# Six edge passes of a graph-transformer kernel: four bf16 products that nobody reads ahead of each chunk's product, sixteen ahead of the first

## The reference, cut to what matters

```python
# layers 0 and 2: attention over edges
msgs = xl[src] * alpha[:, :, None]
out = jax.ops.segment_sum(msgs, dst, num_segments=n)
# layer 1, twice
msg = ew[:, None] * h[src]
agg = jax.ops.segment_sum(msg, dst, num_segments=x.shape[0])
# layer 3, three times (widths 256, 512, 256)
msg = h[src] * norm[:, None]
agg = jnp.zeros_like(h).at[dst].add(msg)
```

## The kernel before

| pass | stands for | columns | beside it |
|---|---|---|---|
| a0 | layer 0 attention | 264 | `l0_queries` |
| c1a | layer 1, first | 256 | layer 1 mixing |
| c1b | layer 1, second | 256 | nothing |
| a2 | layer 2 attention | 272 | `l2_mix` |
| d3a | layer 3, first | 256 | `l3_mix` |
| d3c | layer 3, second | 512 | nothing |
| d3e | layer 3, third | 256 | nothing |

## Time and profile before

### The profile page before, as it was taken

One profiled execution on the slowest core, in us unless ns is written; L12 is line 12 of the kernel. 1 busy time (PEld: TensorE's weight loads), 2 busy tenths in 40 slices (PEclk: granted clock), 3 DMA queues, 4 the chain that ended last, 5 costly groups with the idle time before them and its releaser, 6 DMA issues.

```text
span 7906.2 us, 73457 instructions
## 1 busy us (share of the span) xinstructions
PE 5426.0 (69%) x20758; PEld 3443.5 (44%) x20758; DVE 4236.9 (54%) x12574; ACT 1138.5 (14%) x2552; POOL 3801.9 (48%) x3736
## 2 busy tenths in 40 slices
PE   4302566655876677776887776666678777777698
PEld 3102453325743333335776443454443224333587
DVE  8713676675254444445288676865533664444411
ACT  1001241111210010002242122110010001000222
POOL 3773026652556636652502666027643664666133
PEclk9998778876977875567988988788889999555799
DMA  2101243334733323334742334023334664333465
GB/s 63 39 3 30 81 134 92 92 71 127 200 93 92 91 66 91 92 74 136 187 135 83 90 88 109 9 62 89 89 72 119 184 181 126 92 92 87 130 196 173
DMA packets 345017, 801.98 MB, mean 101 GB/s; under 512 B 96963, under 2 KB 196807, under 8 KB 331845
## 3 DMA queue, kind: packets, MB, share of 16 engines
q0 software_dynamic: 202752, 491.35, 24.2%
q1 hardware_dynamic: 141872, 305.94, 12.4%
HBM read 722.42 MB, written 77.80 MB: 101 GB/s over the span
## 4 chain that ended last, share of the span: by engine, by line
PE 41%; DVE 16%; DMA 10%; issue 9%; POOL 6%; another core or an unknown queue 4%; DVEq 1%; ACT 1%; POOLq 0%; SPq 0%; PEld 0%; PEldq 0%; ACTq 0%
PE bank L2138 20%; DMA arena<-TAB,arena 6%; POOL arena L2121 5%; PE bank L1402 4%; PE bank L1388 4%; DVE arena L2182 4%; PE bank L341 3%; DVE arena L2171 2%; DVE arena L2440 1%; PE bank L1615 1%; PE bank L1604 1%; DVE arena L2161 1%; DMA SUM<-arena 1%; DVE arena L228 1%
## 5 line engine op out<-in xcount | busy, mean ns | idle before, releaser
L2138 PE MATMUL bank<-arena 128*125 128x256 f32 (+3 forms) x5824 | 2658.8, 565 | 1183.8 <-DMA arena<-TAB,arena 262.7
L2121 POOL DMA_INDIRECT arena<-TAB,arena x2080 | 1991.5, 957 | 1672.0 <-DMA TAB<-arena 652.8
L2138 PEld LDWEIGHTS bank<-arena 128*125 128x125 f32 x5824 | 1186.8, 243 | 2603.2 <-issue 921.6
L2182 DVE TENSOR_TENSOR arena<-bank,arena 125x256 f32 (+3 forms) x2912 | 1351.4, 464 | 1524.5 <-PE bank L2138 966.3
L2121 POOL DMA_INDIRECT arena<-TABa,arena x832 | 865.0, 1040 | 1162.4 <-DVEq L141 774.4
L2161 DVE TENSOR_SCALAR arena<-arena 128x125 f32<-128x125 f32 x2080 | 616.9, 297 | 275.1 <-PE bank L2138 140.6
L1739 POOL DMA_INDIRECT REC<-arena x400 | 427.8, 1070 | 230.4 <-issue 121.6
L1343 POOL DMA_INDIRECT SUM<-arena x192 | 307.4, 1601 | 459.1 <-DVE arena L1553 391.6
L341 PE MATMUL bank<-arena 128*125 128x256 f32 (+4 forms) x1600 | 455.7, 433 | 89.2 <-DVE arena L2278 24.2
L1388 PE MATMUL bank<-arena 128*128 128x256 f32 x2048 | 465.3, 383 | 7.0 <-DVE arena L1541 4.8
L1402 PE MATMUL bank<-arena 128*128 128x256 f32 x2048 | 463.9, 383 | 0.0
(11 more groups left out here) (506 smaller groups left out, 5651.6 us busy)
## 6 DMA issues: line engine op xcount, KB each, us to landing
arena<-L_ffn_pack SPq DMA_DIRECT2D x32, 2054.0 KB
arena<-L_ffn_pack SPq DMA_DIRECT2D x64, 1026.0 KB
arena<-TAB,arena POOLq DMA_INDIRECT x2080
arena<-SLR SPq DMA_DIRECT2D x52, 512.0 KB, 3.7
arena<-DLR SPq DMA_DIRECT2D x52, 512.0 KB, 4.8
arena<-TABa,arena POOLq DMA_INDIRECT x832
arena<-L_ffn_b SPq DMA_DIRECT2D x96, 128.0 KB
arena<-LROW SPq DMA_DIRECT2D x20, 610.4 KB
```

The lines of the kernel that those rows point to most:

```text
L2121: e.indirect_dma_start(out=m.G[k % m.ring][:, 0:m.width], out_offset=None, in_=m.table[:, :], in_offset=bass.IndirectOffsetOnAxis(ap=eidx[ ...
L2138: e.matmul(ps[0:P, 0:m.full], m.S[k % SRING], m.G[k % m.ring], start=True, stop=True).then_inc(*put("pass_p", m.g, "summed", k))
L2182: e.tensor_tensor(o, banks.of(m.g, "added", k)[0:P, 0:m.full], o, ALU.add).then_inc(*put("pass_v", m.g, "added", k))
```

## The change

In six of the passes (all but the one of 512 columns) TensorE now computes further products between its wait for the bank and its wait for the chunk's matrix and rows: sixteen for the first chunk, four for each other. They are bf16, 128 rows by 256, 248 or 240 columns, each with its own loading of 128x128 weights; both operands are the bytes of constants that never change (`ident`, `ones` and what follows, read as bf16). They write the columns of the same bank that the chunk's fp32 product leaves free, which nobody reads, and signal no semaphore. In d3c no column is free, and nothing is added.

```diff
+    STEADY, FIRST = 4, 16
+    keepw, keepx = at(K0, 128, p=128, dt=BF16), at(K0, 256, p=128, dt=BF16)
+
+    def keep_pe(e, m, ps, k):
+
+        w = min(256, 512 - m.full)
+        if w < 128:
+            return
+        for _ in range(FIRST if k == 0 else STEADY):
+            e.matmul(ps[:, m.full:m.full + w], keepw, keepx[:, 0:w], start=True, stop=True)
+
     def pass_pe(e, m, steps=None, room=None):
         upto = beside(steps)
         for k in range(KC):
...
             if before:
                 e.wait_ge(*of(*before))
+            keep_pe(e, m, ps, k)
             e.wait_ge(*of(m.g, "onehot", k))
             if m.heads:
                 e.wait_ge(*of(m.g, "extra", k))
```

## The result

The changed kernel takes 7248.52 us (median of 6 runs, 7222.65 to 7261.45) beside 7198.32 us for the kernel before on the same chip (6 runs, 7190.85 to 7215.84). The ratio is 1.0065, 95% interval 1.005 to 1.0079: 36 to 57 us slower, about 47. The forecast was 7226 us, with a range of 7150 to 7320.

What follows compares the result with a forecast made beforehand. The prediction took GpSimd's gathers, 1.25 us a chunk, to bound the passes, not TensorE. Terms +20 (a2), +10 (d3a), +5 (a0), -5 (behind the passes) made +30 on the median 7196: 7226 us, range 7150 to 7320.

Steps and rivals of the forecast that it cites:

- The clock: In all six changed passes TensorE would run at the high clock, as in d3c at 0.96; 0.9 or more expected.
- Rival 4: The clock stays low: 241 us more in each of c1b and d3e, 7680 us or above; chance 0.05.
- c1b and d3e, cost 0: In c1b and d3e TensorE's 0.91 us a chunk hides under the 1.25 us gathers; cost 0, gain 0.
- The sixteen, cost 0: The first chunk's sixteen products, 1.7 us or 3.4 at the low clock, run while TensorE awaits the first rows; cost 0.
- a2, +20, and d3a, +10: GpSimd's waits beside side work grow by half in a2, +20 us, and by a third in d3a, +10 us.
- The 96% load: In a2 TensorE would need 538 of 559 us, chunks and side work together.
- rival 2: TensorE becomes the bound in a2 and d3a: a2 +70, d3a +40, a0 +20 us, 7326 us; chance 0.10.
- a0, +5, and c1a, 0: Waits beside side work grow by a quarter in a0, +5 us, and not at all in c1a.
- Behind the passes, -5: After c1a, c1b and d3a the next step's transposes and products start at the high clock; -5 us in all.
- The premise on the profiler: The 75 us of standstills a pass, 525 of the profiled span's 710 us excess, are mostly a cost of being profiled.
- Rival 3: Unprofiled gathers come faster, so the low clock's 0.98 us a chunk binds c1b and d3e; faster, 7133 us; chance 0.15.
- Rival 1: All of it is hidden, passes a0 to d3e keep their length; 7196 us, within 14 us; chance 0.25.

Runs made afterwards that it cites:

- experiment 9: Kernel before with a deeper ring in d3e alone (twelve gather buffers for six, eight of S for four, one-hots six chunks ahead): 7208.85 us beside 7209.79.
- experiments 3 and 4: One kernel run twice: the added products in c1b and d3e alone; against the kernel before, 7917.94 us (1.0051) and 7973.58 us (1.0066).
- 5: The added products in a2 and d3a alone; 7924.35 us beside 7882.90 for the kernel before, 1.0058.
- 7 and 8: Added products in a0, c1a, a2 and d3a only, in chunks near a side-work step, then only in the others; against kernel before 1.0063 and 1.0061.
- 6: The changed kernel with eight added products a chunk instead of four, in all six passes; 8143.95 us beside 7882.90 for the kernel before, 1.0337.
- experiment 12: Changed kernel without added products in a2's chunks near a side-work step, and four instead of sixteen at a0's first chunk; 7201.34 us, kernel before 7201.46.
- experiment 1: The kernel before profiled once more, no edit; 7884.08 us beside 7882.90, 0.9997.

## Why the prediction was right, point by point

**The clock.** Predicted high in all six passes, read from d3c. It is 0.98 to 0.99, c1b from 0.61 in the kernel before of the same condition:

```profile
924.00:1466.00 542.00, 397.65 (x1062) 206.91 (x1062) 409.92 (x1275) 93.15 (x445) 411.23 (x416) 0.82 0.43 108
2583.00:3103.00 520.00, 423.83 (x821) 188.50 (x822) 281.78 (x820) 0.00 (x0) 393.12 (x416) 0.61 0.38 104
3869.00:4413.00 544.00, 435.32 (x1532) 263.27 (x1532) 443.21 (x1470) 134.20 (x640) 417.13 (x416) 0.95 0.42 109
```

(a0, c1b and a2 of experiment 9.) Rival 4 is out. The likeness to d3c held: TensorE is busy 436 of 520 us in c1b after and 441 of 521 in d3c, both at 0.99. The busy share alone would not have told it, since c1b before had 424 of 520 at 0.61.

**c1b and d3e, cost 0.** This holds to 0.4 us in c1b, and in d3e there is no difference (519.0 before and after). The timeline of after in c1b:

```profile
2849.93 0.67 PE L2150 MATMUL bank<-arena 128*125 128x256 f32 x2 [0.16 <-DVE arena L2194]
...
2850.44 0.60 PE L2134 MATMUL bank<-arena 128*128 128x256 bf16 x4
...
2850.84 0.95 POOL L2121 DMA_INDIRECT arena<-TAB,arena  x1 [0.30 <-PE bank L2150]
...
2852.09 0.95 POOL L2121 DMA_INDIRECT arena<-TAB,arena  x1 [0.30 <-PE bank L2150]
```

The gathers start 1.25 us apart, 0.30 us after the end of the one before. The pass's own product now takes 2850.44 - 2849.93 = 0.51 us where the earlier trace rows gave 0.98, and no gather waited for it beyond its 0.30 us. TensorE is busy 436 us of the 520, 1.05 a chunk, a little over the 0.91 of the forecast, since that was for products without a pause and these come in two pieces whose ends count (0.60 and 0.67 us in the rows, 0.44 and 0.47 in the forecast). The prediction read one thing wrong that does not change its sum: the 590.3 us of d3c in the earlier trace rows count 412 of its 416 gathers (and the a0 and d3a there 415). The whole pass is

```profile
L2121 POOL DMA_INDIRECT arena<-TAB,arena x416: 940/946/997, 6034.1 to 6629.4; - x139
```

which is 595.3 us beside c1b's 595.0, so the two clocks make no difference. The whole a0 is 616.5 us and d3a 623.2, so 3 and 1 us more of their own than the prediction took.

The Trainium skill, "TensorE: Matmul & The Clock Gate", section "Why this matters for your kernels", advises keeping TensorE continuously busy for its clock. The six passes agree, at 0.98 to 0.99 with their pauses partly filled. Another stretch of before, transposes and products of 8 columns behind a0, does not: TensorE counts there as busy without a pause, at 0.50:

```profile
1827.50:1855.00 27.50, 27.50 (x134) 27.50 (x134) 6.80 (x27) 7.18 (x13) 0.00 (x0) 0.50 0.00 1
```

That a higher clock pays is what c1b's 519.4 and 519.0 us deny, since its bound is GpSimd.

**The sixteen, cost 0.** a0's first gather starts at 924.2 us in experiment 9 and 924.7 after, and the first gathers of c1b follow each other by 1.25 us. It holds.

**a2, +20, and d3a, +10.** Measured +24 and +5 to +9. The 96% load was right: 543.66 of 568 us. Gather by gather, a2 after falls behind experiment 9 by 1 us up to the 78th gather, by 20 from there to the 312th, and by 3 in the rest. Where the load gathers is seen in 52 us in the middle of a2, after first and then experiment 9 at about the same chunks (from the 122nd and the 125th):

```profile
4060.00:4112.00 52.00, 52.00 (x305) 38.36 (x305) 37.56 (x128) 9.65 (x48) 36.50 (x37) 1.00 0.37 97
```

```profile
4040.00:4092.00 52.00, 43.79 (x168) 27.46 (x166) 42.84 (x150) 11.45 (x60) 39.66 (x40) 1.00 0.40 105
```

TensorE is busy 52.00 of 52 us, and 37 gathers pass instead of 40. The stream there, after, PE alone:

```profile
4104.23 1.13 PE L341 MATMUL bank<-arena 128*125 128x256 f32 x4
4105.20 0.57 PE L2134 MATMUL bank<-arena 128*128 128x240 bf16 x4
4105.61 0.63 PE L2150 MATMUL bank<-arena 128*125 128x272 f32 x2
...
4107.82 1.03 PE L955 MATMUL bank<-arena 125*128 125x257 f32 x4
...
4109.31 1.13 PE L341 MATMUL bank<-arena 128*125 128x256 f32 x4
4110.27 0.57 PE L2134 MATMUL bank<-arena 128*128 128x240 bf16 x4
```

From L2134 at 4105.20 to L2134 at 4110.27 it takes 5.07 us for three chunks (0.87 each) and the side work between them (2.45 us), 1.69 us a chunk, where GpSimd would issue one each 1.25. In experiment 9 the same cycle takes 4.41 us, 1.47 a chunk, with a pause in it:

```profile
4071.56 1.03 PE L955 MATMUL bank<-arena 125*128 125x257 f32 x4
...
4075.44 0.69 PE L2139 MATMUL bank<-arena 128*125 128x272 f32 x2 [0.35 <-DVE arena L2172]
```

(the next L955 starts at 4075.97). That too is over 1.25, and yet no gather stands there for more than its 0.30 us, so the delay stayed within what the nine buffers cover. After, it doesn't, and GpSimd has to stand:

```profile
4106.51 1.21 POOL L2121 DMA_INDIRECT arena<-TABa,arena  x1 [0.98 <-PE bank L2150]
...
4111.58 1.21 POOL L2121 DMA_INDIRECT arena<-TABa,arena  x1 [1.36 <-PE bank L2150]
```

Who waits for whom in a2 says the same, after and then experiment 9 (waiter, awaited: us in total, times, longest):

```profile
POOL arena L2121 <- PE bank L2150: 65.0, 155, 3.2
```

```profile
PE bank L2139 <- DVE arena L2172: 95.2, 196, 5.3
...
POOL arena L2122 <- PE bank L2139: 38.2, 125, 0.4
```

Before, GpSimd's 125 waits for the product L2139 were the fixed 0.30 us each (38.2 us, longest 0.4), and TensorE itself waited 95.2 us for VectorE's L2172. These waits of TensorE were the room that the four products took, and more than it: GpSimd's waits go to 65.0 us with 3.2 the longest. Less the fixed 0.30 each (155 x 0.30 = 46.5) that is 18.5 us of waiting, most of the 24. In dense stretches the mechanism is thus rival 2's (TensorE is the bound), in size the forecast's, because the dense stretches are a part of the pass.

That the sizes came out near is in part luck. The prediction let waits of 40 us in a2 and 28 in d3a, read with the standstills of the other condition taken off at 75 us a pass, grow by half and by a third. Beside 519 us the kernel before has 25 and 37 us of its own in the forecast's condition (543.6 and 556.0), and these grew to about double and by a fifth.

**a0, +5, and c1a, 0.** -2 and +2 us, and in two further profiles +1 and +2 (a0), +1 and +3 (c1a), at a load of 88 and 89%. The term for a0 was too high.

**Behind the passes, -5.** -3.0 us behind c1a, -0.5 behind d3a, 0 behind c1b.

**What failed: the stretch from a0 to c1a.** The sum gave it nothing, and it has 23 of the 50 us. In it lies the feed-forward part of layer 0, with the same instructions as before. GpSimd's line L1343 there, which adds results into SUM by indirect DMA, in experiment 9 and after (busy and mean; idle before it and its releasers):

```profile
L1343 POOL DMA_INDIRECT SUM<-arena x64 | 102.6, 1603 | 81.2 <-DVE arena L1553 60.8 <-issue 9.9 <-DMA SUM<-arena 9.8
```

```profile
L1343 POOL DMA_INDIRECT SUM<-arena x64 | 102.6, 1603 | 103.7 <-DVE arena L1553 65.4 <-DMA SUM<-arena 24.4 <-issue 13.0
```

It waits 24.4 instead of 9.8 us for earlier sums to land, so the gathers of XNT queued behind it are late, and TensorE waits for these 28.4 us in place of 15.9, the longest 6.7:

```profile
PE bank L1373 <- DMA arena<-XNT,arena: 15.9, 4, 6.6
```

```profile
PE bank L1373 <- DMA arena<-XNT,arena: 28.4, 7, 6.7
```

The products of the feed-forward part (first L1388 to last L1402), after and then experiment 9, show how much of the stretch this is:

```profile
1635.00:1909.40 274.40, 250.37 (x1148) 214.79 (x1148) 70.48 (x189) 62.01 (x129) 156.43 (x120) 0.94 0.71 184
```

```profile
1634.80:1886.60 251.80, 241.63 (x1147) 210.44 (x1148) 69.94 (x187) 61.90 (x129) 156.30 (x120) 0.98 0.76 200
```

They take 22.6 of the 23 us more: TensorE idles 24.0 us instead of 10.2, and is busy 8.7 us longer for the same products, at a granted clock of 0.94 instead of 0.98.

The cause stays open. The stretch (one profile each) takes 498 to 504 us in four profiles of before, and 520 to 523 in three of the change. With the products in part of the passes it takes 509.1 and 504.7 (experiments 3 and 4, nothing changed ahead of it), 516.2 (5, the same), 504.2 and 502.8 (7 and 8, a third and two thirds of a0's added products ahead of it), 519.4 (6) and 518.0 (12). So work left over from a0 doesn't explain it, nor does the mere number of instructions ahead. Nor is the wait for the sums enough: it is 24.5 us in experiment 4 too, where the stretch is 504.7 us, and in the feed-forward part between c1b and a2 it grows from 12.7 to 25.1 us while that stretch stays at 766.9 and 766.8.

**The premise on the profiler was wrong**: 75 us a pass are found in timed runs as in profiled ones, in one condition and not in the other, and a profiled execution of experiment 9 (7195.8 us) is as short as the timed ones. It did no harm to the forecast only because the sum was set against the median, which was in the condition without standstills. Rival 3, which wanted the low clock to bind in timed runs, fell with it.

**The total.** +30 was forecast, about +47 measured. The terms that the sum had, +35 in the passes and -5 behind them, measured +30 and -3 in the table; the excess is the unforeseen stretch, about as large as the whole +20 for a2. Rival 1 is true of a0, c1a, c1b and d3e and false of a2 and d3a. Of a2's part experiment 12 shows the cause by taking it away; its time, equal to that of before, says that the rest can go as well, and not how.

## What to carry to other kernels

Work that keeps an engine's clock up is free only under a bound that lies elsewhere, and it pays only where someone waits for that engine; look at the gathers' spacing first. Where an engine works through its stream in order and has side work in it, compare its time per chunk within the densest stretch, not over the pass: 96% over a2 was 100% over 52 us. And a profile far from the median of the timed runs may come from another condition than they; find out before its excess is explained away.

## What the runs showed of the hardware that was not expected

- The same kernel took 7882.90 and 7917.48 us on two chips and 7198.32, 7209.79 and 7201.46 on three other occasions. The difference of about 700 us lies in all seven passes (590 us against 519 for c1b, d3c and d3e) and in the preparation (first gather at 1128.0 us in experiment 1, 924.2 in experiment 9).
- In the longer condition an edge pass with nothing beside it grows by 14 to 17 us when four products a chunk are added (experiments 3 and 4); in the other it keeps its 519 us.
- At nearly one busy share of TensorE in the profile, 424 and 436 us of 520, the granted clock was 0.61 and 0.99 (c1b before and after).
- bf16 products of 256 columns, each with its own weights, pass at 109 ns each (0.87 us for eight), the same per column as the 85 ns of 200 columns in the earlier trace rows.
